# When VectorE reduces the adjacency tiles and builds the index lists of a sparse graph attention: a new order of the same work

## The reference, cut to what matters

```python
q = query @ Wq.T + bq
k = key @ Wk.T + bk
v = value @ Wv.T + bv
scores = jnp.einsum('nd,md->nm', q, k) / 4096 ** 0.5
adj_scores = scores * adj_matrix
adj_scores = jnp.where(jnp.abs(adj_scores) < 1e-05, -1e9, adj_scores)
prob = jax.nn.softmax(adj_scores, axis=-1)
y = jnp.einsum('nm,md->nd', prob, v) @ Wm.T + bm
out = layernorm(x + y)
```

## Time and profile before

| | us |
|---|---|
| median of 3 runs | 456.69 (456.53 to 458.04) |
| the profiled execution | 457.7 |
| its span (first to last instruction) | 455.9 |
| PE busy | 434.3 (95%) |
| DVE busy | 315.7 (69%) |
| ACT busy | 190.6 (42%) |
| POOL busy | 166.9 (37%) |

### The profile page before, as it was taken

The page is one execution under the profiler, slowest core; times in us unless marked ns, Lnnn a source line. Parts: engine busy times, 40 slices in busy tenths (PEclk is TensorE's granted clock), DMA queues, the critical chain, the costliest instruction groups (busy, mean ns, idle before and its releaser), DMA issues.

```text
span 455.9 us, 5475 instructions
## 1 busy us (share of the span) xinstructions
PE 434.3 (95%) x1536; PEld 245.8 (54%) x1536; DVE 315.7 (69%) x923; ACT 190.6 (42%) x448; POOL 166.9 (37%) x180
## 2 busy tenths in 40 slices
PE   8999999999999987999978999999999999999982
PEld 5344444444444444565645666666656666666651
DVE  0348553797546807798999898887986886557675
ACT  1233422333333243434335536454454544554573
POOL 3100000002352046265653564555545354463300
PEclk9999999999999999899999999999999999999997
DMA  8999999999999999999999996799968749665643
GB/s 325 380 226 265 287 282 294 213 281 266 295 321 329 374 259 288 268 297 293 325 254 227 328 321 209 290 286 260 397 216 280 250 148 307 209 198 177 178 148 118
DMA packets 32452, 121.58 MB, mean 267 GB/s; under 512 B 5080, under 2 KB 5336, under 8 KB 30370
## 3 DMA queue, kind: packets, MB, share of 16 engines
q0 software_dynamic: 16240, 72.79, 61.1%
q1 hardware_dynamic: 12866, 28.51, 17.0%
q10 hardware_dynamic: 3312, 19.89, 11.0%
HBM read 139.78 MB, written 17.56 MB: 345 GB/s over the span
## 4 chain that ended last, share of the span: by engine, by line
PE 83%; DVE 10%; ACT 3%; issue 2%; DMA 1%; DVEq 0%; ACTq 0%
PE bank L558 24%; PE bank L568 21%; PE bank L686 11%; PE bank L710 10%; PE bank L668 6%; PE bank L609 3%; PE bank L621 3%; PE bank L697 2%; PE bank L677 1%; DVE big L1049 1%; DVE stats L1268 1%; ACT keyT L894 1%; DMA qT<-wmT 1%; DVE big L1051 1%; DVE score L1233 1%
## 5 line engine op out<-in xcount | busy, mean ns | idle before, releaser
L568 PE MATMUL bank<-big,M 128*128 128x472 f32 (+1 forms) x288 | 122.6, 553 | 0.3 <-ACT y_buf L831 0.3
L476 POOL DMA_INDIRECT v_g<-table,index x70 | 70.8, 1011 | 119.3 <-PE bank L710 97.3
L558 PE MATMUL bank<-y_buf,big 128*128 128x512 f32 x256 | 111.6, 594 | 0.7 <-ACT y_buf L853 0.7
L466 POOL DMA_INDIRECT key_adj_g<-key_adj,index x70 | 72.6, 1037 | 21.3 <-issue 21.3
L558 PEld LDWEIGHTS bank<-y_buf,big 128*128 128x128 f32 x256 | 48.1, 190 | 59.4 <-issue 57.9
L568 PEld LDWEIGHTS bank<-big,M 128*128 128x128 f32 x288 | 52.5, 192 | 46.9 <-issue 44.7
L686 PE MATMUL bank<-keyT,qT 128*118 128x256 f32 x280 | 67.2, 383 | 6.8 <-DVE score L1226 5.0
L1049 DVE TENSOR_TENSOR big<-big 128x1888 bf16<-128x1888 bf16 x35 | 39.8, 1137 | 42.3 <-DMA big<-adj_tiles 42.3
L686 PEld LDWEIGHTS bank<-keyT,qT 128*118 128x118 f32 x280 | 50.6, 182 | 29.5 <-issue 16.8
L457 POOL DMA_DIRECT2D big<-adj_tiles x35 | 19.8, 567 | 124.5 <-PE bank L558 78.3
L710 PE MATMUL bank<-v_g,probT 128*118 128x512 f32 x136 | 64.0, 593 | 0.5 <-ACT probT L920 0.5
(11 more groups left out here) (122 smaller groups left out, 470.9 us busy)
## 6 DMA issues: line engine op xcount, KB each, us to landing
big<-adj_tiles POOLq DMA_DIRECT2D x35, 944.0 KB, 13.2
x_buf<-x SPq DMA_DIRECT2D x35, 256.0 KB, 5.6
out<-y_buf SPq DMA_DIRECT2D x34, 256.0 KB, 5.5
big<-valueT ACTq DMA_DIRECT2D x8, 1024.0 KB, 11.0
big<-xT SPq DMA_DIRECT2D x7, 944.0 KB, 10.6
table<-qT ACTq DMA_DIRECT2D x5, 1024.0 KB, 14.7
table<-y_buf ACTq DMA_DIRECT2D x3, 1024.0 KB, 15.2
big<-xT ACTq DMA_DIRECT2D x2, 944.0 KB, 9.1
```

What stands on the lines that cost most here:

```text
L466: pool.indirect_dma_start(key_adj_g[:, b, c, :], None, key_adj, bass.IndirectOffsetOnAxis(index[:, t, CH + c:CH + c + 1], 0),).then_inc(ke ...
L476: pool.indirect_dma_start(v_g[:, b, c, :], None, table, bass.IndirectOffsetOnAxis(index[:, t, c:c + 1], 0), bounds_check=N - 1, oob_is_err ...
L558: mm = nc.tensor.matmul(bank[4 + t % 2][:, :], col_buf[nb % 2][:, d, k * P:(k + 1) * P], G[:, d, :], start=(d == 0), stop=(d == DC - 1))
L568: mm = nc.tensor.matmul(ps[:, 0:n], M[:, d, a * P:(a + 1) * P], xT_buf[nb % 2][:, d, 0:n], start=(d == 0), stop=(d == DC - 1))
```

## The change

One tree more, that of tile 19, runs ahead of the main loop: the loop there still covers tiles 0 to 18, and `reduce_tile(19)` follows `key_bias(0)`, so it stands between the preparation and `soften(0)`. Trees 20 to 23 then come at tiles 0 to 3, 24 to 31 at tiles 8 to 15, 32 to 34 at tiles 20 to 22. The lists of batches 2, 3 and 4 start at tiles 4, 16 and 23 (before: 5, 13 and 21). Within a tile the tree now stands ahead of `index_slots`. POOL's order ahead of the loop stays (tiles 19 to 22); in the loop the loads follow `trees_of`, three tiles ahead of their trees.

```diff
-        FIRST = 19
-        TREES = ({0: [FIRST, FIRST + 1]} | {i: [FIRST + i + 1] for i in range(1, 8)}
-                 | {i: [FIRST + i] for i in range(9, 13)} | {i: [FIRST + i - 4] for i in range(17, 20)})
-        LIST_AT = {2: 5, 3: 13, 4: 21}
+        FIRST = 20
+        TREES = ({i: [FIRST + i] for i in range(4)} | {i: [FIRST + i - 4] for i in range(8, 16)}
+                 | {i: [FIRST + i - 8] for i in range(20, 23)})
+        LIST_AT = {2: 4, 3: 16, 4: 23}
...
             for t in range(3, KD):
                 gather_keys(t)
+            load_adj(FIRST - 1)
             for i in range(3):
                 for t in trees_of(i):
                     load_adj(t)
...
-            for t in range(FIRST):
+            for t in range(FIRST - 1):
                 reduce_tile(t)
...
             key_bias(0)
+            reduce_tile(FIRST - 1)
...
                 if i == T:
                     last_statistics(T - 1)
+                for t in trees_of(i):
+                    reduce_tile(t)
                 if step == STEPS - 1:
                     index_slots(b)
-                for t in trees_of(i):
-                    reduce_tile(t)
                 if step == 0:
```

## The result

The changed kernel takes 454.05 us (median of 20 runs), the kernel before in the same comparison 457.48: the ratio is 0.9929, 95% interval 0.9914 to 0.9945, a gain of 3.2 us (the two medians differ by 3.4). The forecast was 449.5 us, 7.2 us faster, with a range up to 452.9; the sign was right, the size was not. Of the 4.6 us between 449.5 and 454.05, 0.8 is the kernel before itself: it came out at 457.48 here, and the forecast started from 456.69. The profiled execution (452.62 us, span 450.7) is one of the quicker of the 20; its span is 5.2 us shorter than that of the kernel before. So nearly 2 us of what the median lacks are in no trace.

The account below looks back on a forecast made before the run. PE was taken to bound the kernel except where it waits for DVE. Terms 2.5 + 1.07 + 5.1 - 1.5 = 7.2 us took the profiled 457.7 us to 450.5, the median to 449.5 us; range 447.6 to 452.9.

Parts of the forecast that it names:

- the loss of 1.5 us at tile 34: Tree 34, due in tile 22, waits 2.7 us for its load; beyond 1.2 us spare, PE loses 1.5 us.
- the 0 for the loads of tiles 24 to 31: Trees 24 to 31 in tiles 8 to 15, one per tile with loads three tiles ahead, cost 0.
- The gains: 2.5 us at tile 1, 1.07 us in the next tile, 5.1 us in tiles 3 to 9; together 8.65 us.
- the late end of tree 19: Ahead of the loop, tree 19 ends at 168.9 to 171.2; the late end costs 0.2 us.
- the +7.8: On POOL, tile 34's load is issued 7.8 us after the transposes of tile 20, behind four gathers.
- the index is ready at +2.8: Batch 3's index, behind tree 32, is ready 2.8 us after the transposes of tile 20.
- 4.2 us: Estimate from the Trainium skill for tile 34's 944 KB load; it would land at +12.0, in time.
- the cover is 23.4: Loads of trees 24 to 31 are issued 23.4 us ahead, covering slower landings of eight in a row; cost 0.
- PE waiting in tiles 8 to 15: Sign of error: PE waits there would mean loads in a row fall behind by more than their cover.
- The rivals: Tile 34 very late: slower, 0.04; tile 34 free: 448.0 us, 0.20; list stretch slow: 454.6 us, within a 0.09 case.
- a late enough load takes the whole gain: Rival at tile 34: landing above 18.9 us makes the kernel slower, 0.04; at 27.4, 466.5 us.
- the 16 us and more that were asked for: Tile 34's load landing in 16.2 to 18.9 us: no measurable difference, chance 0.05; above 18.9, slower.

Follow-up runs that it names:

- spread_and_34: loads_spread with the loads of tiles 32 to 34 one POOL step earlier, that of 34 ahead of tile 24's key gather; 449.14 us, ratio 0.9823 to the kernel before.
- load34_early: The changed kernel with tile 34's load at POOL's step 18, ahead of the key gather of tile 24; 450.44 us, ratio 0.9846 to the kernel before.
- loads_spread: The changed kernel with loads of tiles 24 to 27 at POOL's steps 1 to 4, 28 to 31 at 9 to 12; 452.29 us, ratio 0.9888 to before.
- load34_late: The changed kernel with tile 34's load moved behind the two key gathers of tile 25 in POOL's queue; 458.46 us, ratio 1.0008 to the kernel before.
- index_first: The changed kernel with one edit undone, index_slots ahead of the tree again; 450.77 us, ratio 0.9844 to the kernel before.
- tree19_only: The kernel before with one edit: tree 19 ahead of the first tile's product, tile 0 with tree 20 alone; 454.13 us, ratio 0.9932.

## Why the prediction was wrong, point by point

Two terms of the sum failed: the loss of 1.5 us at tile 34 was too small, and the 0 for the loads of tiles 24 to 31 was not 0. The gains were right. In the working of tile 34 the four gathers with the 0.1 us before them are 5.0 us, not 4.9 (the +7.8 has it right), and the late end of tree 19 is 171.1, not 171.2; neither moves the sum.

**Right: the gains.** Forecast 8.65 us. The change's trace has 2.69 + 1.04 by tile 2 and 8.80 by tile 9; spread_and_34 keeps them to the end (8.83 in its trace, 8.1 by its ratio, with 8.65 in the interval). Tree 19 fitted into the idle time: it started at 165.05, when its load landed after 26.1 us, and `soften(0)` at 171.03 as before:

```profile
165.05 1.14 DVE L1050 TENSOR_TENSOR big<-big 128x1888 bf16<-128x1888 bf16 x1 [6.23 <-DMA big<-adj_tiles]
...
171.03 0.48 DVE L1228 SCALAR_TENSOR_TENSOR score<-bank,c_cols,adjT 118x256 f32<-118x256 f32 x1 [2.69 <-PE bank L687]
```

The granted clock in 184 to 186 us is 1.00 instead of 0.50:

```profile
184.00:186.00 2.00, 2.00 (x14) 1.49 (x13) 1.90 (x5) 0.91 (x2) 0.00 (x0) 1.00 1.01 225
```

**Right in mechanism, too small: tile 34.** The step was "So the index is ready at +2.8. [...] the load is issued at +7.8." The rest of that term held: it took 9.8 us (taken: 10.4) and DVE's spare time was 3.81 - (10.76 - 8.23) = 1.28 us (taken: 1.2). But the index came at +3.4, the first gather only 0.4 us behind it, two of the gathers took 1.20 and 1.71 us where 1.0 was put, and the load went out 1.8 us later than forecast. Forecast loss 1.5, in the profiled execution 2.5; the faster landing hid 0.6 of the 1.8. By the ratios it is more: 3.8 us from load34_early against the change, 3.0 from spread_and_34 against loads_spread, where 2.5 is at the edge of what the first allows and within the second. The landing of this load took 9.8, 11.6, 11.0 and 10.0 us in the four traces in which it stood behind the gathers, each of another kernel (the change, loads_spread, load34_late, index_first), and beyond the spare time each microsecond is paid: in loads_spread 5.58 us of waiting cost 12.54 - 8.23 = 4.31. A landing of 11.1 us would give the loss of 3.8 (an estimate from these numbers). Whether the longer executions of the change had it, and why the landing varies, stays open.

The Trainium skill's figure for such a transfer (DMA: Bandwidth & Descriptors, "Anatomy of one DMA — SWDGE (gpsimd) path"), from which 4.2 us were estimated, is not borne out here: the four took 9.8 us and more.

**Wrong: "Their loads are issued three tiles ahead [...] the cover is 23.4."** The loads of adj had that cover, and no tree of tiles 24 to 31 waited. The error was to ask only whether the moved transfers were in time, and not whom they hold up. SP's load of x that tile 11 uses has some 12 us between issue and use (246.36 to 258.5, where L1172 would have begun), and took 14.1; PE waiting in tiles 8 to 15 was named as a sign of error, but without a price. It costs 0.94 us in the change's trace (8.86 - 7.92), and by the ratios 1.9 from the change against loads_spread and 1.1 from load34_early against spread_and_34; the last alone is not clear of the noise.

The kernel before was in time by little. Its load for the same use was issued at 254.78 and landed after 11.2 us, 1.3 us ahead of L1171 (267.30):

```profile
254.78 0.34 SPq L409 DMA_DIRECT2D x_buf<-x  x1
...
267.30 0.74 DVE L1171 CUSTOM_DVE_ANT_0 big<-x_buf,w_row,kappa 118x512 f32<-118x512 f32 x1
```

The stretch just before the issue differs between the change and loads_spread, which loads no adj tile there; the DMA share is in the last column but one:

```profile
230.00:238.00 8.00, 8.00 (x34) 5.00 (x33) 5.60 (x22) 4.57 (x10) 4.64 (x6) 1.00 1.03 284
```

```profile
230.00:238.00 8.00, 8.00 (x34) 5.00 (x33) 5.64 (x22) 4.57 (x10) 4.03 (x5) 1.00 0.57 175
```

An xT load that SP issues behind this stretch, at 240.07 and 240.96, took 18.2 us in the change and 7.5 in loads_spread. Which of the eight adj loads hold x up is not shown; by tree19_only it does not take all of them.

The Trainium skill has the rule for it (DMA: Bandwidth & Descriptors, "Issuing engines are not separate DMA queues"): transfers issued by different engines run on the same sixteen DMA engines and interleave. The trace agrees: POOL's loads spread out, and the x loads of SP land after 8.3 us (median of four) instead of 12.2.

Together, in the traces: 8.83 us gained (spread_and_34), 2.53 lost at tile 34 (10.76 - 8.23) and 0.94 in tile 11, which leaves the 5.36 that the change's trace has. By the ratios 8.1 - 3.8 - 1.1 = 3.2, but that sum cannot fail, since each term is the step from one of these kernels to the next; by loads_spread the same steps are 3.0 and 1.9. Against the forecast of 7.2 they make the missing 4.0: the gains 0.6 short, and 3.4 more lost at the two places together.

**The rivals.** None of the three came about in the change. That a late enough load takes the whole gain was right as a mechanism: load34_late is at 1.0008, though it got there with a landing of 11.0 us, by being issued later and by the slow matmuls behind the idle stretch, not with the 16 us and more that were asked for. The turn of the sign beyond that is not shown.

## What to carry to other kernels

When work is moved to a later place, look at the queue in which its consumer waits, and price everything behind that wait up to the next deadline: here one load behind one waiting gather took back 3 to 4 of 8.1 us, and placing it one step earlier, or the index one tree earlier, returned it. A transfer moved into a full stretch is to be charged with what it does to the transfers of other engines that have the least time between issue and use. In spread_and_34 the loads of tiles 24 to 31 go out when their buffers come free, not a fixed distance ahead of their use, and that of tile 34 ahead of the waiting gather; its trace has neither wait and no new one.

## What the runs showed that was not expected

A gather that starts on POOL while L1050, the first instruction of a tree, runs on DVE takes longer: the second value gather of the change took 1.71 us at 343.22, beside L1050 from 342.92 to 344.05, and the first key gather of index_first 1.62 us at 336.63, beside L1050 from 336.27; the median of the key gathers is 0.96. In the change's trace from 160 us on, ten of the eleven gathers that start while L1050 runs took 1.28 to 1.77 us; those that start before it and run into it took 0.96 to 1.05. The reason is not shown. Here a tree in the tile made POOL's queue slower just when it was catching up.

PE can pay for an idle stretch twice: in load34_late a wait of 7.61 us on DVE cost 15.86 - 8.23 = 7.63 us, with none of the 1.28 us of spare time that showed at the smaller waits: at a granted clock of 0.50 the scores behind the stretch took 3.74 instead of 1.96 us. The length of the one wait does not settle it: after 3.52 us in loads_spread the clock stayed at 1.00, and in the kernel before it fell to 0.50 behind a wait of 2.24 us. What decides is not shown.
